# An AdaLN block with a top-2 mixture of experts: one region of rows for each expert, slots in an order made on the chip, and the mixing behind the FFN loop

## The chip, the cores and the metric

The kernel runs on one core of one Trainium2 chip. The metric is the device time of one execution in microseconds (us), as the median of several runs. The engines are named as in the profile: PE is TensorE (PEld its weight loads), DVE is VectorE, ACT is ScalarE, POOL is GpSimd, and SP is the queue that issues most of the DMAs.

## The reference

32 batches of 256 tokens (8192 in all) with 128 features go through a layer norm with a shift and scale from `c`, linear attention over 32 features, a gated residual, a second norm, a mixture of experts, and a second gated residual. Eight experts have 512 hidden units each; every token takes the two with the largest gate values. Cut to what matters:

```python
mod = (_silu(c) @ wmod).reshape(32, 6, 1, -1)        # sa, ca, ga, sb, cb, gb
h = _layernorm(x) * (1 + ca) + sa
x = x + ga * attention(h)                            # linear attention with a causal sum over 256 tokens
h = _layernorm(x) * (1 + cb) + sb
gate = softmax(h @ w_gate.T)                         # 8 experts
scores, idx = top_k(gate, 2)
cw = (one_hot(idx, 8) * scores[..., None]).sum(axis=1)
y = einsum('teh,ehd->ted', gelu(einsum('td,edh->teh', h, W1) + b1), W2) + b2
x = x + gb * einsum('ted,te->td', y, cw)
```

## The kernel before

The program is written out engine by engine, with semaphores; no scheduler moves anything. It has three stages.

**Attention.** `steps` (L235) runs 19 software-pipelined steps, one for each pair of batches (`PAIRS` = 16, four tiles of 128 tokens in a pair) plus the ends of the pipeline. A step `p` does the first half of pair `p`, the second half of `p - 1`, and the second norm, gate logits and fp16 rows of `p - 2` (POOL's part, the fold of the gates into `MEMO` and `GA`, is done once at L471 to L479). In eight of the steps the expert weights are split into two fp16 parts as well (`weights_high`, `weights_low`).

**Routing.** The pairs fall into three groups (`GPAIRS` = 7, 5, 4). When the last logits of a group are there, `steps` calls `route(g)` on PE, ACT and DVE. On DVE (L866 to L923) it finds the two experts of each token, gets from PE the rank of every token within its expert (`upper` and `onesh`, L1187 and L1188), lays the slots out and writes two tables: `POS`, the row in the slot buffer for each token and choice, and `EXPT`, the expert of each slot. A slot is 256 rows of one expert. Each group has its own buffer, in which every expert begins a new slot, so a group needs 7 slots more than its rows fill: `ST` = 35, 27 and 23, together `SLOTS` = 85. POOL then scatters the rows of the group into the buffer with one indirect DMA for each tile and choice (`scatter`, L496, 128 in all). The buffers were cleared beforehand by SP (`clear`, L378).

**FFN and mixing.** All engines run `ffn_loop` (L255) over the 85 slots. For a slot, SP loads it transposed (`load`, L344), PE multiplies by W1 (`up`, L1201), ACT applies gelu (L655), DVE splits the result into two fp16 parts (`split`, L1000 and L1002), PE multiplies by W2 (`down`, L1213), DVE adds the bias (`rows`, L1011) and SP stores the slot (`store`, L355). The slots stand in the order of the groups. When all slots of a group are stored, POOL gathers its rows back, in chunks of four tiles, 8 indirect DMAs to a chunk (`gather`, L500, 16 chunks). Chunk `c` goes to place `c % 8` of a ring of eight, so a gather from chunk 8 on waits for the mixing of chunk `c - 8` (L503). DVE mixes a chunk with three or four instructions of 512 or 1024 elements (`mix`, L1014): the first four chunks (`MIXED`) inside the FFN loop, the others behind it, with ACT doing the scaling (L670). SP writes each mixed chunk out.

```python
ST = tuple(2 * TOK * n // SLOT + E - 1 for n in GT)          # L23: 35, 27, 23
MIX0 = S0[1] // BODY + 2                                     # the turn of the loop with the first mixing
for g in range(GROUPS):                                      # POOL, L525
    for k in range(RING):
        pool.wait_ge(y_out[k], 16 * stored(k, S0[g + 1]))    # all slots of the group are stored
    for c in range(G0[g] // CH, (G0[g] + GT[g]) // CH):
        gather(c, g)
```

## Time and profile before

| | us |
|---|---|
| median of 3 runs | 536.07 (535.74 to 537.32) |
| the profiled execution, its own time | 537.64 |
| its span in the trace | 535.9 |
| busy in the span: PE, DVE, ACT, POOL | 375.2, 444.0, 333.8, 316.4 |
| chain that ended last: PE, DVE, ACT, without a visible wait, POOL | 52%, 22%, 10%, 8%, 3% |

The page's table of stages (busy tenths in 40 slices of 13.4 us) shows DVE at 8 or 9 tenths up to about 235 us, PE at 9 or more from there to about 470 us, and PE at 0 in the last five slices, while POOL stays at 7 or 8 tenths from 335 us to the end. The granted clock of PE is 10 tenths of full speed in the FFN loop and 6 to 9 tenths before it. Busy shares over the whole span mix the three stages; a change is read in the stage that it touches.

### The profile page before, as it was taken

The page shows a single profiled execution, that of the slowest core. Times are in us where ns is not written, and L with a number is a line of the kernel's source. Part 1 is how long each engine was busy: PE and PEld are TensorE (multiplying, and loading weights), DVE is VectorE, ACT ScalarE, POOL GpSimd, SP SyncE. Part 2 cuts the span into 40 slices and gives each one's busy share as a digit, 9 for nine tenths or more (in the row PEclk, how much of TensorE's full clock was granted, in tenths as well). Part 3 has the DMA queues.
Part 4 walks back from the last instruction along what each step waited for, and adds up shares of the span by engine and source line. Part 5 has one row for each costly group of instructions (what it writes and reads, how often), then busy time and mean ns, then how long its engine had stood idle before and what let it go on. Part 6 is the DMA issues. An engine that isn't in the chain of part 4 may idle for free.

```text
span 535.9 us, 14939 instructions
## 1 busy us (share of the span) xinstructions
PE 375.2 (70%) x4184; PEld 333.8 (62%) x4185; DVE 444.0 (83%) x1042; ACT 333.8 (62%) x746; POOL 316.4 (59%) x343
## 2 busy tenths in 40 slices
PE   3846537682877567269999999999999999920000
PEld 3635537570766366149989999999999899820000
DVE  6889998899999877559888899999999999975314
ACT  2634638993899464356767777766776667794111
POOL 2228500000777777677777700578888888887774
PEclk9987668986798767579999999999999999975555
DMA  8896004552557513726565533465555555365232
GB/s 217 233 378 185 1 0 124 157 161 83 152 184 209 169 52 83 211 80 134 145 144 142 144 96 96 124 146 133 137 131 139 127 136 138 107 191 142 69 91 70
DMA packets 129696, 73.19 MB, mean 137 GB/s; under 512 B 53760, under 2 KB 123008, under 8 KB 129408
## 3 DMA queue, kind: packets, MB, share of 16 engines
q1 hardware_dynamic: 121472, 56.02, 37.8%
q0 software_dynamic: 8192, 16.79, 12.1%
q8 instruction: 14, 0.23, 0.2%
q14 instruction: 18, 0.15, 0.1%
HBM read 21.75 MB, written 34.90 MB: 106 GB/s over the span
## 4 chain that ended last, share of the span: by engine, by line
PE 52%; DVE 22%; ACT 10%; issue 8%; POOL 3%; ACTq 1%; DMA 1%; DVEq 1%; SPq 0%; POOLq 0%
PE psA L1213 22%; PE psA L1201 11%; PE psV L1201 5%; PE psH L1201 5%; POOL ROW L511 3%; DVE ATT L771 3%; ACT ROW L670 2%; DVE stats L710 2%; PE psH L1110 2%; DVE w_parts L946 1%; ACT ATT L610 1%; DVE X L847 1%; PE psA L1119 1%; PE psA L1121 1%; PE psA L1120 1%
## 5 line engine op out<-in xcount | busy, mean ns | idle before, releaser
L511 POOL DMA_INDIRECT ROW<-slot_out,POS x128 | 152.7, 1193 | 67.8 <-issue 63.8
L496 POOL DMA_INDIRECT slot_rows<-ROW,POS x128 | 131.2, 1025 | 96.0 <-DVE EXPT L923 53.6
L1213 PE MATMUL psA<-WST,ATT 128*128 x2040 | 136.7, 220 | 1.7 <-DVE ATT L1002 1.7
L1213 PEld LDWEIGHTS psA<-WST,ATT 128*128 128x128 f16 x2040 | 123.8, 98 | 10.0 <-issue 2.3
L1002 DVE SCALAR_TENSOR_TENSOR ATT<-ATT,f_scales 128x1024 f16<-128x1024 f32 x85 | 109.1, 1284 | 3.0
L655 ACT ACTIVATE ATT<-psA,b1T,f_scales 128x256 f32<-128x256 f32 x172 | 83.1, 564 | 33.8 <-PE psA L1201 32.5
L1000 DVE TENSOR_SCALAR ATT<-ATT,f_scales 128x1024 f16<-128x1024 f32 x85 | 64.6, 760 | 8.6 <-ACT ATT L655 5.0
L1201 PE MATMUL psA<-WT,WST 128*128 128x256 f16 x516 | 64.8, 276 | 5.4 <-DVE RT L911 3.0
L655 ACT ACTIVATE ATT<-psV,b1T,f_scales 128x256 f32<-128x256 f32 x84 | 42.9, 561 | 36.3 <-PE psH L1201 35.6
L1201 PEld LDWEIGHTS psA<-WT,WST 128*128 x516 | 48.2, 99 | 13.5 <-issue 6.8
L1110 PE MATMUL psH<-ident,ATT 128*128 128x128 f32 x64 | 14.8, 373 | 54.6 <-DVE ATT L771 54.6
L1011 DVE SCALAR_TENSOR_TENSOR VP<-psA,f_scales,b2B 128x256 f32<-128x256 f32 x85 | 40.9, 481 | 10.6 <-PE psA L1213 8.1
L1110 PEld LDWEIGHTS psH<-ident,ATT 128*128 128x128 f32 x64 | 9.4, 184 | 62.4 <-DVE ATT L771 50.0
L670 ACT ACTIVATE ROW<-ROW,CW x88 | 26.2, 396 | 31.9 <-POOL flag L521 31.9
L655 ACT ACTIVATE ATT<-psH,b1T,f_scales 128x256 f32<-128x256 f32 x84 | 42.8, 567 | 0.0
L1201 PE MATMUL psV<-WT,WST 128*128 128x256 f16 x252 | 34.8, 275 | 0.0
L1028 DVE TENSOR_TENSOR ROW<-ROW x15 | 10.3, 689 | 29.6 <-ACT ROW L670 29.6
L1201 PE MATMUL psH<-WT,WST 128*128 128x256 f16 x252 | 34.4, 273 | 0.0
L597 ACT ACTIVATE ATT<-psH,modT 128x256 f32<-128x256 f32 x32 | 16.3, 558 | 19.8 <-PE psH L1110 19.8
L610 ACT ACTIVATE ATT<-X,shift,rstd 128x128 f32<-128x128 f32 (+1 forms) x64 | 26.1, 479 | 1.5 <-DVE shift L725 1.5
L1201 PEld LDWEIGHTS psH<-WT,WST 128*128 x252 | 24.7, 98 | 2.9
L1201 PEld LDWEIGHTS psV<-WT,WST 128*128 x252 | 23.3, 99 | 2.2
(202 smaller groups left out, 695.3 us busy)
## 6 DMA issues: line engine op xcount, KB each, us to landing
slot_out<-VP SPq DMA_DIRECT2D x85, 128.0 KB
slot_rows<-zero SPq DMA_DIRECT2D x9, 1024.0 KB, 5.6
X<-in_x SPq DMA_DIRECT2D x8, 512.0 KB, 7.0
WST<-in_W SPq DMA_DIRECT2D x2, 2048.0 KB, 14.7
WST<-WT SPq DMA_DIRECT2D x16, 256.0 KB
...
slot_rows<-ROW,POS POOLq DMA_INDIRECT x128
...
```

The costliest lines, as they stand in the source:

```text
L496: nc.gpsimd.indirect_dma_start(xg[g], bass.IndirectOffsetOnAxis(ap=POS[:, k * TILES + t:k * TILES + t + 1], axis=0), ROW[:, t * 2 * D:(t + ...
L511: nc.gpsimd.indirect_dma_start(YG[:, o:o + D], None, yg[g], bass.IndirectOffsetOnAxis(ap=POS[:, i:i + 1], axis=0)).then_inc(done, 16)
L597: last = nc.scalar.activation(H2T[:, b * SEQ:(b + 1) * SEQ], psH[:, b * SEQ:(b + 1) * SEQ], ACT.Identity, bias=modT[:, ds(3 * BATCH + 2 * ...
L610: last = nc.scalar.activation(XN[:, 1 - j, t * D:(t + 1) * D], X[:, ds((p + 1) * PT * D + t * D, D)], ACT.Identity, bias=shift1[:, ds((p + ...
L655: last = nc.scalar.activation(G[:, k % 2, m * SLOT:(m + 1) * SLOT], psU[k % 2][m // 2][:, m % 2 * SLOT:(m % 2 + 1) * SLOT], ACT.Gelu, bias ...
L670: done = nc.scalar.activation(y, y, ACT.Copy, scale=CW[:, k, ds(c * CH + t, 1)])
L1000: nc.vector.tensor_scalar(GH[:, k % 2, :], G[:, k % 2, :], f_scales[:, 3:4], None, ALU.mult).then_inc(ghigh_ready, 1)
L1002: nc.vector.scalar_tensor_tensor(out=GL[:, k % 2, :], in0=G[:, k % 2, :], scalar=f_scales[:, 3:4], in1=GH[:, k % 2, :], op0=ALU.mult, op1= ...
L1011: nc.vector.scalar_tensor_tensor(out=halves(YR[:, k, :]), in0=halves(psD[k % 2][:, 0:SH * D]), scalar=f_scales[:, 4:5], in1=bias, op0=ALU. ...
L1110: last = nc.tensor.transpose(psH[:, t * D:(t + 1) * D], XN2[:, t * D:(t + 1) * D], ident[:])
L1201: last = mm(o, W1S[:, ds(e * 2 * FF + a * FF + m * 128, 128)], XT[:, k, b * SLOT:(b + 1) * SLOT], start=(c == 0), stop=(c == 2))
L1213: last = mm(psD[k % 2][:, h * D:(h + 1) * D], a[:, k % 2, i:i + TOK], W2S[:, ds(e * 2 * FF + b * FF + m * D, D)], start=(m == 0 and c == 0 ...
```

## The change

- One DRAM buffer holds a region of 33 slots for every expert (`REGION`), for all tokens. A token's row in its expert's region is its rank over all tokens so far (`ends` carries the counts from group to group). Only the last, partly filled slot of each expert is cleared (eight DMAs with an address from a register, issued by SP at its slot 4), and one spare slot at the buffer's end; the clearing of whole buffers (`clear`, 12 DMAs) goes.
- Four groups of four pairs (`GPAIRS` = 4, 4, 4, 4) in place of three, so four calls of `route`. After a group, the slots that are full by then are numbered in the order (row of slots, expert); the last group also takes the partly filled ones. The order is cut at `S0` = 0, 9, 25, 41, 71: 71 slots in place of 85. The tables `EXPT` and `BLOCK` (which slot of the buffer) come from ranks and one-hot products on PE.
- `NEED[c]` is the number of slots that must be stored before chunk `c` can be gathered. POOL reads the 16 numbers into registers after the last scatter and waits, chunk by chunk, on `y_kept`, which SP raises when it has seen a store land (`kept`, two iterations of its loop after the store was issued).
- The gather ring grows from 8 chunks to 16 (the rows' own tile `ROW` and a new tile `BIG`, in which earlier short-lived tiles now lie), so a gather no longer waits for mixing.
- All mixing stands behind the FFN loop: ACT scales the first choice (4 instructions a chunk in place of 8), DVE adds the second with four `scalar_tensor_tensor` of 128 elements, then the gate and the residual as before.
- The constants for the slot order begin with an iota that is now POOL's first instruction and that DVE's first instruction waits for; 15 small POOL instructions (`cells`) follow the fold.

The core of the diff:

```diff
-    GPAIRS = (7, 5, 4)
+    GPAIRS = (4, 4, 4, 4)
-    ST = tuple(2 * TOK * n // SLOT + E - 1 for n in GT)
-    S0 = tuple(sum(ST[:g]) for g in range(GROUPS + 1))
+    MAXC = TILES * TOK // SLOT
+    REGION = MAXC + 1
+    S0 = (0,) + tuple(2 * TOK * PT * n // SLOT - (E - 1) for n in PAIRS_TO[:-1]) + (2 * TOK * TILES // SLOT + E - 1,)
...
 SP:
-    clear(p - LOOPED)
+    if t == RING:
+        sp.wait_ge(table_ready, GROUPS)
+        sp.load(tails, TAIL[0:1, 0:E])
+        for e in range(E):
+            tail = sp.snap(tails[e], min_val=0, max_val=SPARE * SLOT - SLOT)
+            sp.dma_start(xg[ds(tail, SLOT), :].rearrange("(t p) d -> p t d", p=128), zeros).then_inc(zeroed, 16)
...
+def kept(t):
+    sp.wait_ge(y_out[t % RING], 16 * (t // RING + 1))
+    sp.sem_inc(y_kept, 1)
+for t in range(SLOTS + LAG + 2):
...
+    if t < SLOTS:
+        load(t)
+    if LAG <= t < SLOTS + LAG:
+        store(t - LAG)
+    if LAG + 2 <= t:
+        kept(t - LAG - 2)
...
 POOL:
+    nc.gpsimd.iota(celli[:, 0:1], pattern=[[0, 1]], base=0, channel_multiplier=1).then_inc(cell_number, 1)
     nc.gpsimd.memset(ones[:], 1.0).then_inc(ones_ready, 1)
...
-    if c >= YRING:
-        pool.wait_ge(mixed, c - YRING + 1)
+    pool.wait_ge(y_kept, needed[c])
...
+    needed = [pool.value_load(NEED[0:1, c:c + 1], min_val=1, max_val=SLOTS) for c in range(CHUNKS)]
...
 DVE:
+    dve.wait_ge(cell_number, 1)
+    nc.vector.tensor_scalar(celli[:, 1:2], celli[:, 0:1], E - 1, None, ALU.bitwise_and).then_inc(expert_found, 1)
     dve.wait_ge(c_exp, 1)
...
+    ge(dve, order_done, g + 1)
+    link(stt(out=picked[:], in0=psH[:, 0:2], scalar=float(until), in1=open_[:], op0=ALU.is_le, op1=ALU.mult))
...
+    ge(dve, rows_done, g + 1)
+    ts(BLOCK[:, S0[g]:S0[g + 1]], psH[0:1, 128:128 + until], float(SPARE), None, ALU.add)
+    nc.vector.tensor_copy(EXPT[:, S0[g]:S0[g + 1]], psH[0:1, 256:256 + until]).then_inc(table_ready, 1)
...
+    ge(dve, scaled, c + 1)
+    for t in range(CH):
+        last = nc.vector.scalar_tensor_tensor(out=y[:, 0, t, :], in0=y[:, 1, t, :], scalar=CW[:, 1, ds(c * CH + t, 1)],
+                                              in1=y[:, 0, t, :], op0=ALU.mult, op1=ALU.add)
...
 PE, in route:
+    pe.wait_ge(open_ready, g + 1)
+    mm(psH[:, 0:2], mask[:], open_[:], start=True, stop=False)
+    mm(psH[:, 1:2], ones[:], open_[:, 0:1], start=False, stop=True).then_inc(order_done, 1)
+    pe.wait_ge(hot_ready, 2 * (g + 1))
...
     pe.wait_ge(rbase_link, g + 1)
+    pe.wait_ge(table_ready, g + 1)
```

POOL, the first instructions after the common start. Before (an ISA row is an instruction without operands of the kernel; `ones`, `ident` and `mask` are constants):

```order
L431 MEMSET ones 128x128
L432 MEMSET ident 128x128
L433 MEMSET mask 128x128
L435 ISA [waits ones_ready]
L435 AFFINE_SELECT ident<-ident 128x128
L437 AFFINE_SELECT mask<-mask 128x128
```

and in the change, first on POOL and then on DVE, whose first row waits for POOL's iota (`cell_number`):

```order
L453 ISA
L453 IOTA celli 128x1
L454 MEMSET ones 128x128
L455 MEMSET ident 128x128
L456 MEMSET mask 128x128
L458 AFFINE_SELECT ident<-ident 128x128 [waits ones_ready]
```

```order
L721 TENSOR_SCALAR celli<-celli 128x1 [waits cell_number]
L723 TENSOR_SCALAR c_den<-c_den 128x32 [waits c_exp]
L724 RECIPROCAL c_den<-c_den 128x32 [waits setup_link]
L725 TENSOR_TENSOR c_silu<-cT,c_den 128x32 [waits setup_link]
L726 MEMSET BIG 128x2064
L750 BN_STATS stats<-X 128x6 [waits x_in0,setup_link]
```

The ISA row that stood behind three memsets and ahead of the first `affine_select` now stands ahead of the iota, and DVE's chain (`c_den`, the memset, the statistics of `x`) stands behind a row that waits for that iota.

DVE, the last call of `route`, from the rank of the tokens on. Before (`slot_ends` are the ends of the experts' slots, L920 to L923 make `EXPT`):

```order
L904 TENSOR_TENSOR RT<-RT,iota_j 128x112 [waits route_step]
L906 TENSOR_REDUCE slot_ends<-RT 128x8 [waits route_step]
L907 SCALAR_TENSOR_TENSOR slot_ends<-ones,slot_ends 128x8 [waits route_step]
L908 TENSOR_TENSOR slot_ends<-slot_ends 128x8 [waits route_step]
L909 SCALAR_TENSOR_TENSOR RT<-slot_ends,RT 128x128 [waits route_step]
L911 TENSOR_TENSOR RT<-psV,RT 128x128 [waits route_step]
L915 TENSOR_TENSOR RT<-RT 128x2x128 [waits rbase_link]
L916 TENSOR_REDUCE RS<-RT 128x2x16 [waits route_step]
L917 CAST POS<-RS 128x2x16 [waits route_step]
L920 TENSOR_TENSOR CMP<-slot_ends,iota_s 128x184
L922 TENSOR_REDUCE iotaf<-CMP 128x23 [waits route_step]
L923 TENSOR_SCALAR EXPT<-iotaf 128x23 [waits route_step]
```

and in the change, from the same place on (`open` marks the slots that are full and not yet taken, `picked` and `numbered` those taken and their numbers):

```order
L945 TENSOR_TENSOR BIG<-BIG,ends 128x128 [waits route_step]
L946 COPY ends<-BIG 128x8x4 [waits route_step]
L947 TENSOR_TENSOR mine<-ends,cell_expert 128x8 [waits route_step]
L949 TENSOR_REDUCE reach<-mine 128x1 [waits route_step]
L950 SCALAR_TENSOR_TENSOR open<-cell_full,reach,begun 128x2 [waits route_step]
L952 TENSOR_TENSOR BIG<-psV,BIG 128x128
L956 TENSOR_TENSOR BIG<-BIG 128x256 [waits rbase_link]
L957 TENSOR_REDUCE RS<-BIG 128x32 [waits route_step]
L958 CAST POS<-RS 128x2x16 [waits route_step]
L962 SCALAR_TENSOR_TENSOR picked<-psH,open 128x2 [waits order_done]
L963 SCALAR_TENSOR_TENSOR numbered<-psH,picked 128x2 [waits route_step]
L965 TENSOR_SCALAR one_hot<-number,numbered 128x30 [waits route_step]
```

Four wide or small rows ahead of L909 are gone and four small ones have come behind L945; behind `POS` the change has two waits for PE, `order_done` at L962 and, after four more rows, `rows_done` ahead of the two that write `BLOCK` and `EXPT` (L972, L973).

DVE, behind the bias of the last slot. Before:

```order
L1011 SCALAR_TENSOR_TENSOR VP<-psA,f_scales,b2B 128x256
L1041 UNCONDITIONAL_BRANCH
L1041 ISA
L1028 ISA [waits scaled]
L1028 ISA
L1028 TENSOR_TENSOR ROW<-ROW 128x512
L223 ISA
L1033 ISA [waits mix_link]
L1033 TENSOR_TENSOR ROW<-ROW,GA 128x512
L223 REGISTER_ALU
L1036 ISA [waits mix_link]
L1036 TENSOR_TENSOR X<-X,ROW 128x512
```

and in the change:

```order
L1092 ISA [waits scaled]
L1092 ISA
L1092 SCALAR_TENSOR_TENSOR ROW<-ROW,CW 128x128
L1092 ISA x2
L1092 SCALAR_TENSOR_TENSOR ROW<-ROW,CW 128x128
L1092 ISA x2
L1092 SCALAR_TENSOR_TENSOR ROW<-ROW,CW 128x128
L1092 ISA x2
L1092 SCALAR_TENSOR_TENSOR ROW<-ROW,CW 128x128
L251 REGISTER_ALU
L1099 ISA [waits mix_link]
L1099 TENSOR_TENSOR ROW<-ROW,GA 128x512
```

The sum of the two choices, one row of 512 elements before, is four rows of 128 elements; the multiplication by the gate and the addition to `X` (L1102) follow as before. The loops here run over 15 chunks in the change, over 11 before.

## Rows read from the trace of the kernel before

**Rows 1.** Busy time by stage: start:end length, PE, PEld, DVE, ACT, POOL, clock, DMA, GB/s
```profile
300.00:340.00 40.00, 40.00 (x532) 37.21 (x530) 36.60 (x44) 28.25 (x59) 6.91 (x8) 1.00 0.41 106
...
473.00:536.00 63.00, 0.12 (x3) 0.00 (x0) 26.59 (x42) 22.11 (x75) 44.60 (x47) 0.53 0.42 113
```

**Rows 2.** Chain that ended last: start us, us, what; two `up` parts, 38 such entries apart
```profile
254.57 1.31 PE psA L1201 x12
...
465.61 1.32 PE psA L1201 x12
```

**Rows 3.** Timeline, the start: start us, us, engine line operation, [idle before <-releaser]
```profile
2.71 0.18 DVE L683 TENSOR_SCALAR c_den<-c_den 128x32 f32<-128x32 f32 x1 [2.57 <-ACT c_den L537]
...
3.89 1.78 DVE L686 MEMSET MEMO<- 128x2064 f32 x1 [0.38 <-issue]
...
6.75 1.65 DVE L710 BATCH_NORM_STATS2 stats<-X 128x6 f32<-128x128 f32 x8 [1.08 <-DMA X<-in_x]
...
10.76 0.28 POOL L435 TENSOR_SCALAR_AFFINE_SELECT ident<-ident 128x128 f32<-128x128 f32 x1 [9.47 <-issue]
```

**Rows 4.** Timeline of DVE at the three calls of `route`
```profile
121.21 0.39 DVE L879 TENSOR_REDUCE RS<-psQK 128x28 f32<-128x224 f32 x1
...
132.44 0.69 DVE L802 TENSOR_TENSOR AM<-psA,mask 128x512 f32<-128x512 f32 x1
...
179.01 0.29 DVE L879 TENSOR_REDUCE RS<-psQK 128x20 f32<-128x160 f32 x1
...
188.41 0.68 DVE L802 TENSOR_TENSOR AM<-psA,mask 128x512 f32<-128x512 f32 x1
...
222.26 0.29 DVE L879 TENSOR_REDUCE RS<-psQK 128x16 f32<-128x128 f32 x1 [0.58 <-issue]
...
227.99 0.28 DVE L904 TENSOR_TENSOR RT<-RT,iota_j 128x112 f32<-128x112 f32 x1
...
229.01 0.29 DVE L909 SCALAR_TENSOR_TENSOR RT<-slot_ends,RT 128x128 f32<-128x128 f32 x1
...
229.33 0.36 DVE L911 TENSOR_TENSOR RT<-psV,RT 128x128 f32<-128x128 f32 x1
...
230.65 0.18 DVE L917 CAST POS<-RS 128x32 uint32<-128x32 f32 x1
```

**Rows 5.** Timeline of PE: the first `up` of the FFN loop
```profile
230.53 2.74 PE L1201 MATMUL psA<-WT,WST 128*128 128x256 f16 x12 [3.04 <-DVE RT L911]
```

**Rows 6.** Page, costliest groups, the scatters: busy us, mean ns | idle before, releaser
```profile
L496 POOL DMA_INDIRECT slot_rows<-ROW,POS x128 | 131.2, 1025 | 96.0 <-DVE EXPT L923 53.6
```

**Rows 7.** Timeline of POOL: the first and the 25th gather
```profile
338.23 0.98 POOL L511 DMA_INDIRECT ROW<-slot_out,POS  x1 [31.26 <-issue]
...
371.66 1.19 POOL L511 DMA_INDIRECT ROW<-slot_out,POS  x1 [0.30 <-issue]
```

**Rows 8.** Timeline of SP: the store of slot 34, the last of group 0
```profile
335.38 0.37 SPq L361 DMA_DIRECT2D slot_out<-VP  x1
```

**Rows 9.** Timeline behind the FFN loop
```profile
472.22 0.94 POOL L511 DMA_INDIRECT ROW<-slot_out,POS  x1 [0.30 <-DMA ROW<-slot_out,POS]
...
473.27 0.48 DVE L1011 SCALAR_TENSOR_TENSOR VP<-psA,f_scales,b2B 128x256 f32<-128x256 f32 x1 [1.78 <-PE psA L1213]
...
475.48 0.69 DVE L1036 TENSOR_TENSOR X<-X,ROW  x1
...
477.85 0.69 DVE L1036 TENSOR_TENSOR X<-X,ROW  x1
...
490.65 0.94 POOL L511 DMA_INDIRECT ROW<-slot_out,POS  x1 [0.30 <-issue]
...
529.60 0.68 DVE L1054 TENSOR_TENSOR ROW<-ROW,CW 128x512 f32<-128x512 f32 x1
...
533.21 0.43 DVE L1062 TENSOR_TENSOR X<-X,ROW 128x256 f32<-128x256 f32 x1
```

**Rows 10.** Timeline of DVE, attention: four instructions of 128 elements
```profile
191.02 1.12 DVE L823 SCALAR_TENSOR_TENSOR ATT<-psA,RC,X 128x128 f32<-128x128 f32 x4
```

More of the change, by code:

```diff
@@ L355, in store @@
[L355 to L369 removed]
+            xgu, ygu = xg.rearrange("(n p) d -> n p d", p=SLOT), yg.rearrange("(n t p) d -> n p t d", p=128, t=SH)
@@ L479, in _ @@
                                         ALU.mult).then_inc(fold_ready, 1)
+            cells = links(pool, cell_link, 0)
+            tt, ts = nc.gpsimd.tensor_tensor, nc.gpsimd.tensor_scalar
+            number_, expert, row, base, hold = (cell[:, k:k + 1] for k in range(5))
+            pool.wait_ge(expert_found, 1)
+            cells(nc.gpsimd.tensor_copy(cell[:, 0:2], celli[:]))
+            cells(tt(row, number_, expert, ALU.subtract))
+            cells(ts(row, row, 1.0 / E, None, ALU.mult))
+            cells(ts(base, expert, float(REGION), None, ALU.mult))
+            cells(tt(base, base, row, ALU.add))
+            for h in range(2):
+                cells(ts(cell_block[:, h:h + 1], base, float(128 // E * h - SPARE), None, ALU.add))
+                for n, rest in enumerate((SLOT, 1)):
+                    cells(ts(cell_full[:, n, h:h + 1], base, float(SLOT), float(128 // E * h * SLOT + rest), ALU.mult, ALU.add))
+            cells(ts(hold, expert, 1.0, None, ALU.add))
+            cells(ts(cell_expert[:], number[:, 0:E], hold, None, ALU.is_equal))
+            cells(nc.gpsimd.memset(begun[:], 0.0))
+            nc.gpsimd.memset(place_of[:], 0.0).then_inc(route_const, 1)
             pool.wait_ge(wb_ready, 1)
@@ new lines, in route @@
+                link(stt(out=numbered[:], in0=psH[:, 0:2], scalar=float(S0[g]), in1=picked[:], op0=ALU.add, op1=ALU.mult))
+                for h in range(2):
+                    ts(one_hot[:, h, 0:until], number[:, S0[g]:S0[g + 1]], numbered[:, h:h + 1], None,
+                       ALU.is_equal).then_inc(hot_ready, 1)
+                link(tt(begun[:], begun[:], picked[:], ALU.add))
+                link(tt(place_of[:], place_of[:], numbered[:], ALU.add))
+                if g == GROUPS - 1:
+                    nc.vector.tensor_copy(TAIL[:].rearrange("p (e o) -> p e o", o=1), ends[0:1, :, CHUNKS - 1:CHUNKS])
@@ L1045, in mix_half @@
+            spread()
+            dve.wait_ge(table_ready, GROUPS)
+            ffn_loop(dve, ((-3, rows, True), (-1, split, False)), {0: find_needs, 2: keep_needs})
+            dve.wait_ge(gb_in, 16)
+            for half, last in enumerate((YRING, CHUNKS - YRING - 1)):
+                with dve.Fori(0, last) as c:
+                    mix(YG[half][:, ds(c * 2 * CH * D, 2 * CH * D)].rearrange("p (k t d) -> p k t d", k=2, t=CH), c + YRING * half)
             def mix_half(h, base):
@@ L1216, in down, with spread, turn_needs @@
                 last.then_inc(down_done, 1)
+            def spread():
+                pe.wait_ge(diag_ready, 2)
+                for h in range(2):
+                    last = mm(psX[:, h * 128:(h + 1) * 128], ones[:], diag[:, h, :], start=True, stop=True)
+                last.then_inc(spread_done, 1)
+            def turn_needs():
+                pe.wait_ge(need_found, 1)
+                mm(psQK[0:1, 0:CHUNKS], need_col[:], ident[:, 0:CHUNKS], start=True, stop=True).then_inc(need_turned, 1)
             for i in range(2):
```

321 lines of the change are left out of this document (161 added, 160 removed).

## The prediction

> **What bounds the kernel now.** I read the busy time by stage first, then the chain of waits, then the timelines around the places that the change touches. In the FFN loop PE is busy 40.00 of 40 us, and behind it 0.12 of 63 [rows 1]: the loop is bound by PE, and the last 62 us of the span hold no matmul. The chain goes from one PE instruction to the next through the whole loop; between two of its entries lie 38 entries of two slots each, (465.61 - 254.57) / 76 = 2.777 us a slot [rows 2]. Behind the loop POOL still gathers and DVE waits for it. Ahead of the loop DVE's own queue sets the pace: the routing calls are unbroken runs of short DVE instructions [rows 4], and what is added there is paid in full. So slots, DVE instructions ahead of the loop, and what is left to do behind it count; busy time of POOL counts only if it ends last.
>
> The profiled execution took 537.64 us for a span of 535.9. The terms below are changes of that span; the median of the runs, 536.07, lies 1.57 under the profiled execution, and I apply the sum to the median.
>
> **The start: +7.0.** POOL's first `affine_select` runs at 10.76 after 9.47 us in which nothing visible holds it [rows 3]; in the order the ISA row stands just ahead of it. In the change that row stands ahead of the iota, POOL's first instruction, so the iota runs about 10.5. DVE's first instruction waits for it, and behind that stands all of DVE's queue: `c_den` moves from 2.71 to about 10.8. The memset ends at 5.67 now, and the statistics then wait for `x` until 6.75; with 8 us more the memset ends at about 13.7 and the statistics begin there, 7.0 later [rows 3]. PE and ACT wait for DVE here. Bounds: nothing, if the 9.47 us is paid at another place than that row, and 8. I take 7.0.
>
> **Four routing calls for three: +13.7.** Now the first two calls hold DVE from 121.21 to 132.44 and from 179.01 to 188.41, 11.23 and 9.40 us, and from the start of the last, 222.26, to PE's first `up` at 230.53 it is 8.27 [rows 4, 5]. All calls of the change have the width of the last one (128). Its way to the end of L911 is 229.33 + 0.36 - 222.26 = 7.43. Four rows ahead of L909 go: 229.01 - 227.99 = 1.02. Four small ones come, about 0.2 each (L917, a small one, takes 0.18): 7.43 - 1.02 + 0.8 = 7.21. `POS` follows 1.14 later, at 8.35, and releases the scatter. Then six small rows, 1.2, an exposed wait for PE's second answer, and two rows that write the tables, 0.4. DVE to PE takes 230.53 - 229.69 = 0.84 [rows 4, 5]; `POS` and the rows ahead of it cover PE's first answer, two small rows cover a part of the second, and I take 0.5 for the rest: 10.45 a call. Three calls in place of two are 31.35 - 20.63 = +10.7. In the last one PE now waits for the tables: 10.45 + 0.84 - 8.27 = +3.0. With both answers hidden it is +11.7, with 2 us exposed in each call +20.
>
> One weight step becomes an ordinary one and a later ordinary one a weight step: nothing. The 15 small POOL instructions stand in a stretch in which POOL only waits for the first routing call (53.6 us of idle time ended by it) [rows 6]: nothing. The clearing DMAs go: nothing, since DVE bounds that stage; the eight small ones and the reading of their addresses stand on SP ahead of the load of slot 4, which has four slots of 2.777 us to arrive. PE's three small products beside the first slots and DVE's tables for `NEED` lie where PE waits for ACT and DVE for PE's first slots: nothing.
>
> **14 slots fewer: -38.9.** 14 x 2.777, on the bounding engine. Four of the 71 stay empty on these inputs (counting the two largest gate values of each token in the reference gives 67 begun slots), but are computed as well.
>
> **Behind the loop: -13.4.** Now the last bias ends at 473.75 and the span at 535.9: 62.15 us. In the change I expect DVE to be the last engine. A chunk takes 477.85 - 475.48 = 2.37 us now, with three instructions of 512 elements, 0.69 each [rows 9]; one becomes four of 128, 1.12 together [rows 10]: 2.37 - 0.69 + 1.12 = 2.80, and 15 of them are 42.0. The two halves of the last chunk take 533.64 - 529.60 = 4.04 and the end 2.26 as before [rows 9]. With 0.4 for the first wait: 48.7. ACT scales with half its instructions.
>
> **Is POOL done by then?** The FFN starts at 230.53 + 7.0 + 13.7 = 251.2 and DVE's last bias ends 243.2 - 38.9 = 204.3 later, at 455.5; chunk 14 has its turn at 455.9 + 14 x 2.80 = 495. Scatters take 1.025 + (96.0 - 53.6) / 127 = 1.36 each [rows 6], 43.5 for a group of 32. Four steps and a call take 222.26 - 188.41 + 10.45 = 44.3 [rows 4], so each group is done when the next `POS` comes, and the last, from 248.3 on, ends at 292. The 16 register loads have no row; I take 0.5 us each, so gathers begin at 300. In the loop one takes (371.66 - 338.23) / 24 = 1.39 [rows 7], so 111 are out at 455.5; behind it, beside mixing, (490.65 - 472.22) / 12 = 1.54 [rows 9], so the last 17 end at 482, 13 us ahead of DVE. The needed slots, from the same count, are 8, 15, 16, 23, 24 and so on, 40 for chunk 8, 63 for chunk 13, 67 for the last two. Slot 63 is stored and seen about five slots after PE begins it, at 251.2 + 68 x 2.777 = 440; POOL reaches chunk 13 at 445. So the waits by chunk hold POOL hardly anywhere, and no gather waits for mixing any more.
>
> Sum: 7.0 + 13.7 - 38.9 - 13.4 = -31.6, so **504.5 us** for the median.
>
> **Rivals.**
>
> *POOL ends last.* It has 13 us in hand, which go if the 17 gathers beside the dense mixing take over 2.3 us each, or if the register loads cost over 1.3 us each. For: gathers do slow down beside mixing, from 1.39 to 1.54 [rows 7, 9]. Against: that is 11%, with DVE mixing without a break. At one gather for each mixed chunk, 2.80, POOL ends at 455.5 + 47.6 = 503, then landing (2), halves and end, 6.3: a span of 511.4, 511.6 for the median. The Trainium skill, "SBUF — State Buffer", "Who interferes with whom", says that a DVE instruction with two SBUF inputs and a GpSimd instruction that reads SBUF lock each other out for a whole instruction. By that rule the change is worse off than before, as its four small sums have two SBUF inputs and follow one another without a gap, and the time would be that of this rival. The trace bears it out only in part, by the 11%. The Trainium skill, "DMA: Bandwidth & Descriptors", "Latency and other measured facts", gives about 600 ns as the least for a register load, an estimate of 9.6 us for the 16; no row here shows one.
>
> *The start costs nothing.* The 9.47 us may be a load that begins with the kernel and that the iota needn't wait for. For: the profile names no releaser. Against: the ISA row moved with the first instruction that seems to need it. 504.5 - 7.0 = 497.5.
>
> *SP's new wait slows the loop, and the kernel gets slower.* `kept` waits for the store issued two iterations before and stands ahead of the next load. From a landing time over two slots, 5.55 us, SP sets the pace at half the landing time. All of the gain is gone at 31.6 / 71 = 0.445 us a slot, a landing of 6.44 us; at 7 us the loop is 71 x 0.72 = 51 longer, 556. Against: the store of slot 34 was issued at 335.38, and the gather that waits for it runs at 338.23 [rows 7, 8], so it landed within 2.85 us, half of what would hurt. For: no gathers ran beside that store.
>
> *The chunks are not released one by one.* If a late slot were needed by early chunks, all 128 gathers would follow the loop: 455.5 + 128 x 1.54 = 653, about 660 at the end. The count of needed slots speaks against it.
>
> **How the numbers follow.** The forecast (DVE's mixing last, the start delayed) has 0.67, POOL last 0.14, the free start 0.13, SP 0.04, the chunks 0.02. Low end: no cost at the start, -7, answers of PE hidden, -2, and 5 for smaller mixing instructions: 490. High end: answers exposed, +6, and POOL last, +7: 517. These hold about 0.85. A difference of over 0.3% is about what a measurement of this kernel can tell from none: faster 0.93, within 0.01, slower 0.06.
>
> **What would show it.** POOL's iota and DVE's first instruction at about 10.5 us; calls of `route` of 10 to 11 us and the first `up` near 251; slots at 2.77 us, the last bias near 455; the first gather near 300 and the last near 482; DVE busy without waiting for POOL from 456 to 498, 2.80 us a chunk. Wrong would be: an iota before 5 us, DVE idle for POOL's flags behind the loop, PE waiting for `XT` inside it.

## The result, and the profile after

The changed kernel takes 501.44 us (median of 4 runs, 500.05 to 502.06) against 535.9 for the kernel before on the same chip (4 runs): a ratio of 0.9355, 95% interval 0.932 to 0.939. The forecast was 504.5, in a range of 490 to 517. The profiled span fell from 535.9 to 499.4, by 36.5 us; the terms below are parts of that. By the medians the gain is 34.5 us: the profiled execution of the kernel before took 1.7 us more than the median here, so the terms together can be that much too large.

Busy time by stage, after (start:end length, PE, PEld, DVE, ACT, POOL, clock, DMA, GB/s), first inside the FFN loop, then behind it:

```profile
330.00:400.00 70.00, 70.00 (x910) 64.06 (x908) 62.73 (x76) 49.13 (x103) 56.29 (x57) 1.00 0.60 143
449.80:499.40 49.60, 0.00 (x0) 0.00 (x0) 41.53 (x98) 12.77 (x44) 22.92 (x24) 0.51 0.42 116
```

The loop is still bound by PE, as in [rows 1]. Behind it DVE is busy 41.53 of 49.60 us, where before it was busy 26.59 of 63 and POOL 44.60: POOL set the end before, DVE does now.

The chain of waits, two `up` parts of PE, 33 such entries of two slots each apart (start us, us, what):

```profile
258.18 1.31 PE psA L1279 x12
...
441.47 1.32 PE psA L1279 x12
```

(441.47 - 258.18) / 66 = 2.777 us a slot, the figure of [rows 2] to the last digit.

The timeline of the start, after, answers to [rows 3]:

```profile
9.02 0.13 POOL L453 IOTA celli<- 128x1 int32 x1 [8.50 <-issue]
...
9.19 0.15 DVE L721 TENSOR_SCALAR celli<-celli 128x1 int32<-128x1 int32 x1 [9.04 <-POOL celli L453]
...
10.45 2.74 PE L1141 MATMUL psX<-c_silu,BIG 128*128 128x32 f32 x12 [10.45 <-DVE c_silu L725]
...
12.54 1.64 DVE L750 BATCH_NORM_STATS2 stats<-X 128x6 f32<-128x128 f32 x8
```

POOL's iota runs after 8.50 us in which the profile names nothing that holds it; DVE's first instruction waits for it, and the statistics begin at 12.54 instead of 6.75.

The timeline of DVE in the first call of `route`, and of the last call's one long gap and PE's first `up`, answers to [rows 4, 5]:

```profile
97.36 0.26 DVE L919 TENSOR_REDUCE RS<-psQK 128x16 f32<-128x128 f32 x1
...
104.63 0.18 DVE L958 CAST POS<-RS 128x32 uint32<-128x32 f32 x1
104.72 0.15 DVE L962 SCALAR_TENSOR_TENSOR picked<-psH,open 128x2 f32<-128x2 f32 x1
...
105.98 0.16 DVE L972 TENSOR_SCALAR BLOCK<-psH 1x9 int32<-1x9 f32 x1 [0.26 <-PE psH L1265]
106.07 0.15 DVE L973 CAST EXPT<-psH 1x9 int32<-1x9 f32 x1
106.33 0.69 DVE L842 TENSOR_TENSOR BIG<-psA,mask 128x512 f32<-128x512 f32 x1
...
236.74 0.29 DVE L931 SCALAR_TENSOR_TENSOR BIG<-BIG 128x128 f32<-128x128 f32 x1 [0.70 <-ACT BIG L681]
```

```profile
245.32 2.74 PE L1279 MATMUL psA<-WT,WST 128*128 128x256 f16 x12 [1.21 <-issue]
```

A call takes 106.33 - 97.36 = 8.97 us (9.01 and 8.87 in the next two). L962, the row that needs PE's first answer, follows `POS` at once; the second answer costs 0.26 us. Only the last call waits for ACT (0.70).

POOL's last scatter, first gather and last gather, and DVE behind the loop, answer to [rows 7, 9]:

```profile
287.01 1.03 POOL L536 DMA_INDIRECT expert_rows<-ROW,POS  x1 [0.30 <-issue]
300.81 0.99 POOL L551 DMA_INDIRECT ROW<-expert_out,POS  x1 [12.77 <-issue]
...
477.20 1.37 POOL L551 DMA_INDIRECT BIG<-expert_out,POS  x1 [0.30 <-issue]
```

```profile
449.27 0.48 DVE L1085 SCALAR_TENSOR_TENSOR VP<-psA,f_scales,b2B 128x256 f32<-128x256 f32 x1 [1.90 <-PE psA L1291]
449.80 1.15 DVE L1092 SCALAR_TENSOR_TENSOR ROW<-ROW,CW  x4
...
452.66 1.14 DVE L1092 SCALAR_TENSOR_TENSOR ROW<-ROW,CW  x4
...
492.51 0.69 DVE L1102 TENSOR_TENSOR X<-X,BIG  x1
493.12 0.68 DVE L1121 TENSOR_TENSOR BIG<-BIG,CW 128x512 f32<-128x512 f32 x1
```

Fifteen chunks take 493.12 - 449.80 = 43.3 us, 2.89 each, and none of DVE's waits among them names POOL, or ACT, which itself waits for POOL's flags: the last gather is issued 15 us ahead of DVE's last instruction on a whole chunk.

So the span's 36.5 us come out as: the start +5.8 (12.54 - 6.75), four calls for three +8.8 (26.85 against 20.63 for the calls inside the attention, 10.87 against 8.27 for the last one to the first `up`), the loop -38.8 (from the first `up` to the end of the last bias 204.4 us instead of 243.2), the tail -12.5 (49.65 us instead of 62.15): -36.7, with 0.2 in the attention steps.

### The profile page after: what moved, and what is told of

The parts are those of the page before. It is cut to its first block, busy times and chain, and to the rows that moved or that the text cites. A ratio compares the mean times of both kernels' runs of the same rounds, so it can differ in the third digit from the quotient of the medians.

```text
span 499.4 us, 13733 instructions
## 1 busy us (share of the span) xinstructions
PE 343.2 (69%) x3736; PEld 304.1 (61%) x3737; DVE 423.0 (85%) x1099; ACT 298.3 (60%) x663; POOL 306.3 (61%) x360
## 3 DMA queue, kind: packets, MB, share of 16 engines
q0 software_dynamic: 8192, 16.79, 12.5%
## 4 chain that ended last, share of the span: by engine, by line
PE 47%; DVE 32%; issue 10%; ACT 6%; DVEq 3%; ACTq 1%; POOL 0%; POOLq 0%
PE psA L1291 20%; PE psA L1279 10%; PE psV L1279 4%; PE psH L1279 4%; DVE ATT L811 3%; DVE stats L750 2%; PE psH L1177 2%; DVE X L887 2%; DVE w_parts L1020 2%; DVE stats L894 1%; PE psA L1186 1%; DVEq L1092 1%; PE psA L1188 1%; PE psA L1187 1%; DVE ROW L1099 1%
## 5 line engine op out<-in xcount | busy, mean ns | idle before, releaser
L536 POOL DMA_INDIRECT expert_rows<-ROW,POS x128 | 130.1, 1016 | 73.3 <-issue 36.6
L1291 PE MATMUL psA<-WST,ATT 128*128 x1704 | 114.0, 220 | 1.8 <-DVE ATT L1076 1.7
L1291 PEld LDWEIGHTS psA<-WST,ATT 128*128 128x128 f16 x1704 | 103.2, 98 | 8.9 <-issue 2.9
L1076 DVE SCALAR_TENSOR_TENSOR ATT<-ATT,f_scales 128x1024 f16<-128x1024 f32 x71 | 91.2, 1284 | 2.5
L551 POOL DMA_INDIRECT ROW<-expert_out,POS x64 | 69.4, 1084 | 29.8 <-issue 27.4
L694 ACT ACTIVATE ATT<-psA,b1T,f_scales 128x256 f32<-128x256 f32 x144 | 69.6, 563 | 27.6 <-PE psA L1279 27.1
L551 POOL DMA_INDIRECT BIG<-expert_out,POS x64 | 69.7, 1089 | 17.7 <-issue 16.5
L1074 DVE TENSOR_SCALAR ATT<-ATT,f_scales 128x1024 f16<-128x1024 f32 x71 | 53.8, 758 | 6.9 <-ACT ATT L694 1.8
L1197 PE MATMUL psV<-GA,ATT 128*128 (+1 forms) x128 | 23.4, 344 | 0.5 <-DVE BIG L805 0.5
L497 POOL TENSOR_TENSOR BIG<-GA,memo 32x128 f32<-32x128 f32 x28 | 13.0, 465 | 16.5 <-issue 14.5
L1197 PEld LDWEIGHTS psV<-GA,ATT 128*128 128x128 f32 x128 | 22.3, 262 | 1.3 <-DVE BIG L805 1.3
```

The costliest lines, as they stand in the source:

```text
L536: nc.gpsimd.indirect_dma_start(xg, bass.IndirectOffsetOnAxis(ap=POS[:, k * TILES + t:k * TILES + t + 1], axis=0), ROW[:, t * 2 * D:(t + 1) ...
L551: nc.gpsimd.indirect_dma_start(YG[c // YRING][:, o:o + D].bitcast(i32), None, yg, bass.IndirectOffsetOnAxis(ap=POS[:, i:i + 1], axis=0)).t ...
L694: last = nc.scalar.activation(G[:, k % 2, m * SLOT:(m + 1) * SLOT], psU[k % 2][m // 2][:, m % 2 * SLOT:(m % 2 + 1) * SLOT], ACT.Gelu, bias ...
L1074: nc.vector.tensor_scalar(GH[:, k % 2, :], G[:, k % 2, :], f_scales[:, 3:4], None, ALU.mult).then_inc(ghigh_ready, 1)
L1076: nc.vector.scalar_tensor_tensor(out=GL[:, k % 2, :], in0=G[:, k % 2, :], scalar=f_scales[:, 3:4], in1=GH[:, k % 2, :], op0=ALU.mult, op1= ...
L1197: last = mm(psV[:, t * D:(t + 1) * D], HT[:, j, t * TOK:(t + 1) * TOK], GA[:, ds((2 * p + t // 2) * D, D)], start=True, stop=True)
```

## The experiments

Each kernel is the changed kernel with one edit, if nothing else is said. Times are medians; a ratio is to the kernel before on the same chip, so the changed kernel stands at 0.9355, and 0.01 of the ratio is 5.4 us. Spans are those of the profiled executions, beside 499.4 for the changed kernel.

### The start: e1_start and e1b_dve_only

```diff
 POOL:
-    nc.gpsimd.iota(celli[:, 0:1], pattern=[[0, 1]], base=0, channel_multiplier=1).then_inc(cell_number, 1)
     nc.gpsimd.memset(ones[:], 1.0).then_inc(ones_ready, 1)
...
+    nc.gpsimd.iota(celli[:, 0:1], pattern=[[0, 1]], base=0, channel_multiplier=1).then_inc(cell_number, 1)
     nc.gpsimd.memset(onesh[:], 1.0).then_inc(iota_done, 1)
 DVE:
-    dve.wait_ge(cell_number, 1)
-    nc.vector.tensor_scalar(celli[:, 1:2], celli[:, 0:1], E - 1, None, ALU.bitwise_and).then_inc(expert_found, 1)
     dve.wait_ge(c_exp, 1)
...
     last.then_inc(w_ready, 1)
+    dve.wait_ge(cell_number, 1)
+    nc.vector.tensor_scalar(celli[:, 1:2], celli[:, 0:1], E - 1, None, ALU.bitwise_and).then_inc(expert_found, 1)
```

e1b_dve_only has the edit on DVE alone.

> The iota of the cells goes behind POOL's ones, masks and their casts, and DVE's instruction on it behind the set-up of the weights, just ahead of the first attention step. Theory (the iota waits for what stands ahead of it on POOL and DVE's whole queue waits for the iota): DVE's first instruction runs near 2.7 us again instead of 9.2, the statistics begin near 6.8 instead of 12.5, and of the 5.8 us some 5 reach the end: about 496.5 us, 0.99 of the change's time. By the prediction's term it would be 7.0 us, 494.5. Rival (the start is hidden behind the loading of x or recovered in the attention steps): 501 us, no difference, with the first up of the FFN still near 245.

> Only DVE's instruction on the cells moves behind the set-up; POOL's iota stays its first instruction, so that ones, and PE's first product, still wait for it (9.1 and 10.5 us in the change). Theory that DVE's queue carries the price: the statistics begin near 6.8 and most of it comes back, 4 to 5 us, about 497. Rival (PE's first product carries it, since DVE needs its result for the modulation before the first step): only 1 to 2 us come back, about 500.

Measured: e1_start 494.51 us, ratio 0.9218 (0.9178 to 0.9257), span 491.7; e1b_dve_only 499.52 us, 0.9303 (0.9265 to 0.9341), span 497.6. By the medians that is 6.9 and 1.9 us less than the changed kernel. Timeline of the start of e1_start:

```profile
6.39 1.64 DVE L748 BATCH_NORM_STATS2 stats<-X 128x6 f32<-128x128 f32 x8 [0.45 <-DMA X<-in_x]
...
10.22 0.28 POOL L457 TENSOR_SCALAR_AFFINE_SELECT ident<-ident 128x128 f32<-128x128 f32 x1 [8.93 <-issue]
```

and of e1b_dve_only:

```profile
6.79 1.65 DVE L748 BATCH_NORM_STATS2 stats<-X 128x6 f32<-128x128 f32 x8 [1.12 <-DMA X<-in_x]
...
9.38 2.74 PE L1141 MATMUL psX<-c_silu,BIG 128*128 128x32 f32 x12 [9.38 <-POOL ident L455]
...
13.15 0.36 DVE L768 COPY modT<-psX 128x192 f32<-128x192 f32 x1 [2.90 <-PE psQK L1143]
```

The delay isn't hidden: undoing it gives 7.7 us of the span. POOL's 8.9 us are still there in e1_start, now ahead of its first `affine_select` as before the change, where nobody waits. The second run corrects the reason: with DVE free and its statistics at 6.79 only 1.8 us come back, because PE's first product waits for `ones` (`ones_ready`, L1139), which POOL fills behind the iota, and DVE, which needs that product before the first step, now waits 2.90 us for it. (The row names `ident`, the next memset, which raises the same semaphore 0.15 us later.) The rival of e1b_dve_only was right. The first `up` of the FFN varies between kernels that don't differ ahead of it: 244.9 to 247.3 in seven profiles without the edit (mean 245.6), 238.0 to 240.1 in the four with it (mean 239.1; three of them are the combinations at the end). By these the start costs 6.5 us.

### DVE's rows ahead of the loop: e7_more_rows

```diff
+    for again in range(6):
         link(stt(out=picked[:], in0=psH[:, 0:2], scalar=float(until), in1=open_[:], op0=ALU.is_le, op1=ALU.mult))
         link(stt(out=numbered[:], in0=psH[:, 0:2], scalar=float(S0[g]), in1=picked[:], op0=ALU.add, op1=ALU.mult))
```

> In each of the four calls of route the two rows on DVE that rank the cells run six times instead of once, with the same values: 10 small rows more a call, 40 in all. Six small rows take 1.0 us in the change, so 1.7 us a call. Theory (what is added to a call on DVE ahead of the loop is paid in full): 4 x 1.7 = 6.8 us, about 508. Rival (the attention steps behind a call catch up, as they did with 0.8 and 1.0 of the start's delay): the last call pays 1.7 and the other three half or less, about 504 to 505.

Measured: 507.93 us, ratio 0.9465 (0.9422 to 0.9509), span 506.0, 6.6 more. The first `up` stands at 251.59, 6.3 later. The rows in the first call:

```profile
105.79 0.15 DVE L963 SCALAR_TENSOR_TENSOR picked<-psH,open 128x2 f32<-128x2 f32 x1
105.98 0.16 DVE L964 SCALAR_TENSOR_TENSOR numbered<-psH,picked 128x2 f32<-128x2 f32 x1
```

Linked rows of two elements follow each other every 0.19 us, so ten are 1.9 us and four calls 7.6; 6.6 of it reached the end. The rival's 3 to 4 us is out: what a call adds on DVE is paid nearly in full. The busy shares alone don't say so: the page of the kernel before has DVE at 8 or 9 tenths only from 13 to about 187 us, not up to 235, and at 5 to 7 tenths from there to the loop.

### The slots: e2_slots85

```diff
-    S0 = (0,) + ... + (2 * TOK * TILES // SLOT + E - 1,)
+    S0 = (0,) + ... + (2 * TOK * TILES // SLOT + E - 1 + 14,)
```

> The change with 85 slots as before: the last group's share of the order grows by 14, which stay empty on these inputs and are computed on the spare block. Theory (PE bounds the loop slot by slot, whatever is in a slot): 14 x 2.777 = 38.9 us more, about 540 us, so that the change without its smaller number of slots would be no faster than the kernel before. Rivals: the empty slots cost less than 2.777, since nothing scatters to them or gathers from them, or more, since from slot 65 on SP waits for the store before (4 us a slot would make it 17 us more still). POOL has 14 us in hand already and gets more, so mixing starts with all chunks but one there.

Measured: 540.09 us, ratio 1.0073 (1.0051 to 1.0095), span 537.2, 37.8 more, 2.70 for each empty slot. More than the whole gain lies in the number of slots: with 85 the change is 0.7% slower than the kernel before. An empty slot costs as much as a full one within 3%, and SP's waits for the store before, which `store` has at every slot from 65 on, don't show in the time of the loop.

### The tail: e5_act_both and e4_mix_in_loop

e5_act_both:

```diff
 ACT:
-    for t in range(CH):
-        y = YG[half][:, ds(c * 2 * CH * D + t * D, D)]
-        done = nc.scalar.activation(y, y, ACT.Copy, scale=CW[:, 0, ds((c + YRING * half) * CH + t, 1)])
+    for k in range(2):
+        for t in range(CH):
+            y = YG[half][:, ds(c * 2 * CH * D + (k * CH + t) * D, D)]
+            done = nc.scalar.activation(y, y, ACT.Copy, scale=CW[:, k, ds((c + YRING * half) * CH + t, 1)])
 DVE:
-    for t in range(CH):
-        last = nc.vector.scalar_tensor_tensor(out=y[:, 0, t, :], in0=y[:, 1, t, :], scalar=CW[:, 1, ds(c * CH + t, 1)],
-                                              in1=y[:, 0, t, :], op0=ALU.mult, op1=ALU.add)
-    last.then_inc(mix_link, 1)
+    nc.vector.tensor_tensor(y[:, 0], y[:, 0], y[:, 1], ALU.add).then_inc(mix_link, 1)
```

> Behind the loop ACT scales both choices of a chunk (8 copies of 128 instead of 4) and DVE adds them in one instruction of 512 instead of four of 128 with a multiplication. Theory (DVE's own instructions bound the tail): a chunk takes about 2.4 us instead of 2.85, 15 chunks 6.8 us less, about 494.7. Rivals: ACT becomes the bound, 8 copies of 0.21 us with a wait for each chunk (no gain if they take over 2.85 us); or POOL's last gathers end it, which are out at 478.6 against DVE's chunk 14 at 483: then 496 or more, and DVE would wait for POOL's flags.

Measured: 493.17 us, ratio 0.9188 (0.9148 to 0.9228), span 491.1, 8.3 less. Behind the loop, POOL's gathers between DVE's rows:

```profile
451.79 0.69 DVE L1092 TENSOR_TENSOR ROW<-ROW  x1
452.14 1.15 POOL L551 DMA_INDIRECT BIG<-expert_out,POS  x1 [0.30 <-issue]
...
452.70 0.69 DVE L1097 TENSOR_TENSOR ROW<-ROW,GA  x1 [0.21 <-DVE ROW L1092]
453.54 0.69 DVE L1100 TENSOR_TENSOR X<-X,ROW  x1
453.60 1.45 POOL L551 DMA_INDIRECT BIG<-expert_out,POS  x1 [0.30 <-issue]
454.15 0.69 DVE L1092 TENSOR_TENSOR ROW<-ROW  x1
```

A chunk takes 454.15 - 451.79 = 2.36 us instead of 2.89. The tail is bound by DVE's own instructions, and ACT had room for four more copies. Gathers get longer beside it (1.15 to 1.45 us here, 1.26 on average behind the loop instead of 1.10), and POOL's last is issued at 477.20, as in the changed kernel.

e4_mix_in_loop (a turn is eight slots; `MIX0` is 4; ACT scales chunk `n - MIX0` in the turn as well, and `mix` is split into the three parts; cut):

```diff
-    with eng.Fori(1, TURNS) as n:
+    with eng.Fori(1, MIX0 if late else TURNS) as n:
         turn(n)
+    if late:
+        with eng.Fori(MIX0, TURNS) as n:
+            turn(n, late=late)
...
+def late_mix(c, k):
+    if k in (1, 3, 5):
+        mix(0, c, c, (1, 3, 5).index(k))
```

> Four of the 16 chunks are mixed inside the FFN loop again, one in each of turns 4 to 7, in three pieces on DVE (1.15, 0.69 and 0.69 us, behind slots 1, 3 and 5 of the turn), scaled by ACT there. DVE is busy 62.7 of 70 us in the change's loop, 0.29 us free in a slot, 2.3 in a turn of eight, against 2.53 for a chunk. Theory (DVE has room in the loop nearly for one chunk a turn, and the tail is DVE's): the tail is 4 x 2.86 = 11.4 us shorter and the loop about 1 to 2 us longer, so about 491.5 us; DVE's last chunk then has its turn near 481, just behind POOL's last gather at 479. Rival (DVE's pieces delay the split that PE waits for, each by its length): the loop grows by up to 10 us and nothing is gained.

Measured: 496.11 us, ratio 0.9255 (0.9221 to 0.9289), span 492.7, 6.7 less and not 10 (5.3 by the medians). From the first `up` to the last bias the loop takes 204.55 us, 0.1 more than without: its room holds four chunks. But DVE then waits for POOL, which the expectation had just ahead: its row names ACT, and ACT's own row ahead of it names POOL's flag. Those two rows, and POOL's gathers in the loop, from 330 to 440 us, in this kernel:

```profile
481.96 1.28 ACT L711 ACTIVATE BIG<-BIG,CW  x4 [10.41 <-POOL flag L568]
...
483.62 1.15 DVE L1104 SCALAR_TENSOR_TENSOR BIG<-BIG,CW  x4 [4.04 <-ACT BIG L711]
```

```profile
L558 POOL DMA_INDIRECT ROW<-expert_out,POS x41 | 51.9, 1266 | 11.6 <-issue 11.0 <-DMA ROW<-expert_out,POS 0.6
L558 POOL DMA_INDIRECT BIG<-expert_out,POS x31 | 37.6, 1213 | 8.7 <-issue 8.4 <-DMA ROW<-expert_out,POS 0.3
```

and in the changed kernel over the same stretch:

```profile
L551 POOL DMA_INDIRECT ROW<-expert_out,POS x43 | 46.3, 1077 | 11.6 <-issue 9.8 <-SPq L405 1.2 <-DMA ROW<-expert_out,POS 0.6
L551 POOL DMA_INDIRECT BIG<-expert_out,POS x36 | 39.5, 1096 | 9.8 <-issue 8.5 <-SPq L405 0.6 <-DMA BIG<-expert_out,POS 0.6
```

A gather takes 1.21 to 1.27 us instead of 1.08 to 1.10 where DVE mixes in the loop. So the mixing is free for PE and dear for POOL, whose last gather is issued at 485.70 instead of 477.20, and it gives back a part at the end.

### The waits: e3_group_waits and e6_kept_at_once

```diff
-    pool.wait_ge(y_kept, needed[c])
+    pool.wait_ge(y_kept, (S0[2], S0[3], 2 * TOK * TILES // SLOT + E - 1, 2 * TOK * TILES // SLOT + E - 1)[c * CH // GT[0]])
```

> POOL's gathers of a chunk wait for constants by group instead of the chunk's own last slot: 25 for chunks 0 to 3, 41 for chunks 4 to 7, 71 for chunks 8 to 15. All else as in the change. Theory (the price of the prediction's rival that chunks are not released one by one): the 64 gathers of chunks 8 to 15 begin near 453 us, behind the last store, and take 1.33 to 1.6 us each, so the last lands near 545 and the end is near 550, about 50 us more than the change and slower than the kernel before. Rival (most chunks need a late slot anyway, so the group's end is no later): under 10 us more.

```diff
-    if LAG + 2 <= t:
-        kept(t - LAG - 2)
+    if LAG <= t < SLOTS + LAG:
+        kept(t - LAG)
```

> SP waits for a store to land right behind issuing it, and not two iterations later. This puts a number on the rival that SP's wait slows the loop. Theory: a store lands about 2.5 us after its issue, SP's own two instructions take 1.2 and 0.4 us, so an iteration of SP takes about 4 us instead of 2.78 and the loop 71 x 1.3 = 90 us more, about 590 us; the waits at a distance of two iterations cost nothing because two slots, 5.55 us, cover the landing. Rival (the loads have four slots in hand and SP catches up): under 10 us more.

Measured, e3_group_waits: 543.63 us, ratio 1.0138 (1.009 to 1.0186), span 541.7, 42.3 more. The gathers of chunks 8 to 15:

```profile
453.02 0.94 POOL L551 DMA_INDIRECT BIG<-expert_out,POS  x1 [33.89 <-SPq L405]
...
534.63 0.94 POOL L551 DMA_INDIRECT BIG<-expert_out,POS  x1 [0.30 <-issue]
```

63 gathers in 81.6 us are 1.295 each, so the end is 6 us nearer than expected; the mechanism is the one expected. The first 16, issued while DVE mixes without a break, take 1.10 us on average; the 47 from 477 us on take 0.95. Waiting by chunk is worth 42 us: without it the change loses to the kernel before, with all its 14 slots fewer.

Measured, e6_kept_at_once: 569.99 us, ratio 1.063 (1.0572 to 1.0687), span 569.3, 69.9 more. The loop takes 272.4 us, 3.84 a slot. SP's waits (total us, times, longest), and its queue in the loop:

```profile
SPq L405 <- DMA expert_out<-VP: 120.5, 69, 3.4
```

```profile
374.14 0.42 SPq L400 DMA_DIRECT2D expert_out<-VP  x1
376.59 1.21 SPq L392 DMA_TRANSPOSE WT<-expert_rows  x1
```

The next load stands behind the store's landing. A store is seen 0.42 + 120.5 / 69 = 2.2 us after its issue on average. In the changed kernel that wait (L405) stands two slots, 5.55 us, behind the store and shows once, for 1.3 us, behind the loop. Apart from it SP waits for stores only in `store` itself (L399), at the last six slots, four of them empty:

```profile
SPq L399 <- DMA expert_out<-VP: 12.2, 6, 3.5
```

### POOL's numbers: e10_one_load

```diff
-    needed = [pool.value_load(NEED[0:1, c:c + 1], min_val=1, max_val=SLOTS) for c in range(CHUNKS)]
+    needed = nc.values_load_multi_w_load_instructions(
+        NEED[0:1, 0:CHUNKS], engines=[mybir.EngineType.Pool], min_val=1, max_val=SLOTS)[1]
```

> POOL reads its 16 numbers of needed slots in one load instead of 16; the bounds of each are still tested. In the change POOL's first gather stands 12.8 us behind its last scatter, of which the last scatter's landing is some 2. Theory (the loads cost about 0.6 us each): 9 us of the gap go, the first gather runs near 292 instead of 301, the last near 468 instead of 477, and the time stays at 501 us since DVE's mixing, not POOL, ends last. Rival 1 (the tests of the bounds, two for each number, are what takes the time): the gap stays near 12. Rival 2 (POOL sets the end after all): the time falls with POOL's last gather, by up to 9 us.

Measured: 501.01 us, ratio 0.9343 (0.9329 to 0.9357), span 499.3: no difference in the time. POOL's first gather:

```profile
294.44 0.98 POOL L551 DMA_INDIRECT ROW<-expert_out,POS  x1 [7.64 <-issue]
```

The gap fell from 12.77 to 7.64, 0.34 us for each of the 15 loads saved, not 0.6. With 16 loads it lies between 11.64 and 12.77 in eight profiles, so 0.27 to 0.34; what is left holds the landing of the scatters, one load and the tests of the bounds, which no run separates. POOL's last gather is issued at 470.89, 6.3 us earlier, and nothing follows from it: POOL doesn't set the end of the changed kernel.

### Together: e8_best4, e9_best3, e12_best2

The edits of e1_start, e5_act_both, e10_one_load, and chunks mixed in the loop as in e4_mix_in_loop but with ACT scaling both choices: `MIX0` is 4 in e8_best4 (four chunks), 3 in e9_best3 (five) and 6 in e12_best2 (two).

> Together: the cells' iota and DVE's instruction on it late, ACT scaling both choices, four chunks mixed in the FFN loop, POOL's numbers in one load. Theory (the parts add up until POOL or the last slot's store ends last): first up near 238, last bias near 442, 11 chunks of 2.36 us behind it would end DVE at 468 and the span at 474; but the two last chunks need slot 67, which is kept near 444, and their 16 gathers of 1.5 us end near 468, so the span is 475 to 478 and the time about 478 us. Rival (what one part gives another takes: mixing in the loop with ACT's 8 copies and two inputs on DVE slows gathers or PE): 484 or more, with slots over 2.8 us or gathers over 1.6.

> As e8_best4, with the mixing in the loop from turn 3 on, five chunks instead of four. Theory (POOL's 16 gathers behind slot 67 end it, not DVE): within 1 us of e8_best4. Rivals: DVE still ends last, then 2.4 us less; or chunk 0 isn't there at turn 3 (near 305 us, its gathers end near 302) and DVE's wait for it stops the loop, then some us more.

> As e8_best4, with only two chunks mixed in the FFN loop, in turns 6 and 7. There the four of e8_best4 made its loop 2.8 us longer and POOL's gathers 1.21 us long instead of 1.08, and POOL ended last, with DVE 5.5 us idle for it. Theory (mixing in the loop pays until POOL ends last): the loop costs 1.4 us, the tail is 12 chunks of 2.36, the halves and the end, 34.7 us, behind a last bias near 446, so a span near 481 and a time near 483 us, with POOL's last gather near 473 and DVE not idle for it. Rival (POOL still ends last, because dense mixing behind the loop slows its gathers anyway): no better than e8_best4, 486 to 488, with DVE idle for a flag.

Measured: e8_best4 487.04 us, ratio 0.9078 (0.9053 to 0.9104), span 485.5; e9_best3 488.06 us, 0.9103 (0.9083 to 0.9123), span 486.0; e12_best2 483.68 us, 0.9042 (0.9026 to 0.9058), span 481.4. DVE's longest waits behind the loop in e8_best4 and in e9_best3, each with its row of the waits (total us, times, longest):

```profile
DVE BIG L1105 <- ACT BIG L713: 5.5, 1, 5.5
```

```profile
DVE BIG L1105 <- ACT BIG L713: 7.6, 1, 7.6
```

and the end of e12_best2 on POOL and DVE:

```profile
473.04 1.24 POOL L558 DMA_INDIRECT BIG<-expert_out,POS  x1 [0.30 <-issue]
...
474.52 0.69 DVE L1115 TENSOR_TENSOR X<-X,BIG  x1
```

My expectation for e8_best4 was 9 us too low. Five of them lie ahead of the last bias, which ends at 447.23 and not near 442: the first `up` stands 2 us later than expected, and the loop takes 2.8 us more than in the changed kernel. The rest lies behind it, where DVE waits for POOL: a gather in the loop takes 1.20 to 1.22 us here instead of 1.08 to 1.10, so 22 of them follow the last bias and not 16. With five chunks DVE waits longer still. ACT scales the chunk that DVE then adds, and itself waits for POOL's flag, so the row that names ACT means POOL. With two chunks POOL's last gather and DVE's last full chunk end within a microsecond, DVE waits for no flag, and the span is the expected 481. This is the fastest version found, 483.68 us, though its interval just overlaps that of e8_best4; the same edits without any mixing in the loop were not run.

## Why the prediction was right, and where it was off

*What bounds the kernel* held: slots, DVE ahead of the loop, and the work behind it. The forecast's -31.6 became -36.5 in the span, and one term makes up the difference of 4.9. That the others add up to nothing is luck: the start cost 1.2 us less than forecast and the work behind the loop 0.9 more.

*The start, +7.0*: 5.8 at the statistics, 6.5 by the runs with and without the edit. The mechanism was half told. The iota ran at 9.02 and not about 10.5, hence the smaller size. "PE and ACT wait for DVE here" is true, but PE would have waited for POOL anyway, since `ones` had moved behind the iota as well (e1b_dve_only). I looked at DVE's queue and not at what else stood behind the iota on POOL; that the price came out near all the same is luck, as both paths hang on one instruction. The rival of a free start is out.

*Four calls for three, +13.7*: this is the mis-sized term; it was +8.8. A call inside the attention took 8.95 us where I took 10.45, the last one 10.87 to the first `up` where I took 11.29. The step that failed is the 7.43 us "to the end of L911", which I took from the last call of the kernel before, the only one there that waits for ACT's `exp` in the middle. Its row in the timeline of DVE before:

```profile
224.63 0.35 DVE L891 SCALAR_TENSOR_TENSOR RT<-RT 128x128 f32<-128x128 f32 x1 [0.78 <-ACT RT L642]
```

With these 0.78 us in it I had the end of `POS` at 8.35 us into a call where it came at 7.45. The other 0.6 is behind `POS`: PE's second answer cost 0.26 instead of 0.5, six small rows 1.0 instead of 1.2, and the rest is rows that overlap (L962 begins 0.09 us before `POS` ends). That such rows are paid in full was right (e7_more_rows).

*14 slots fewer, -38.9*: -38.8 in the profile, and 37.8 when they were put back.

*Behind the loop, -13.4*: -12.5. A chunk takes 2.89 instead of 2.80, 1.3 us over fifteen, less the 0.4 that I had put down for a first wait that didn't come. That DVE's instructions set this time is shown by e5_act_both.

*POOL done in time*: it was, at 478.6 (forecast 482), from a first gather at 300.81 (forecast 300). A load saved gave back 0.27 to 0.34 us (e10_one_load), where I took 0.5. By the Trainium skill, "DMA: Bandwidth & Descriptors", "Latency and other measured facts", with at least about 0.6 us for one, the 15 loads saved would have given back an estimated 9 us; the traces gave 4.0 to 5.1, and the measurement decides.

*The rival "POOL ends last"* didn't come, though it lies near: e4_mix_in_loop and two of the combinations ended on POOL. The price I had put on it, one gather for each mixed chunk, was wrong. Behind the loop of the changed kernel POOL issues two gathers for each mixed chunk:

```profile
456.87 0.69 DVE L1099 TENSOR_TENSOR ROW<-ROW,GA  x1 [0.21 <-DVE ROW L1092]
457.06 1.32 POOL L551 DMA_INDIRECT BIG<-expert_out,POS  x1 [0.31 <-issue]
...
458.38 1.16 DVE L1092 SCALAR_TENSOR_TENSOR ROW<-ROW,CW  x4
458.69 0.95 POOL L551 DMA_INDIRECT BIG<-expert_out,POS  x1 [0.30 <-issue]
```

A gather that starts inside a row of 512 elements, with over 0.13 us of it left, loses the rest of that row and no more: the one at 457.06 ends at 458.38, 0.82 us behind the end of L1099 at 457.56, and so do the two of e5_act_both above (0.81 and 0.82). Behind the loop in nine of the profiles 107 of 108 such gathers end 0.81 to 0.82 us after the row; a gather beside an idle DVE takes 0.94 to 0.96 from its start. Beside the four small sums, which the prediction named, the row at 458.69 takes no longer than that. So beside the mixing a gather grew by at most 0.5 us, less than one row of 0.69. The Trainium skill, "SBUF — State Buffer", "Who interferes with whom", has a DVE instruction with two SBUF inputs contend with POOL's reads, through shared ports that it calls an exclusive lock. The traces agree, with one instruction as the most that a gather loses; I had made a whole chunk of it. That the second SBUF input is the cause isn't shown, as no run took it away; in the loop, the 51 gathers that start inside the first row of `split` (L1074), which reads one large tile and not two, wait for its end in the same way.

*SP's wait* and *the chunks*: both mechanisms exist, with 70 us (e6_kept_at_once) and 42 us (e3_group_waits) where their conditions were made true, and neither was near: the landing of 2.2 us is a third of the 6.44 from which the first decides.
